# GNN edge stage: first layer summed transposed in one PSUM bank, node sums turned to 24×128

## What is computed

```python
m_input = jnp.concatenate([node_states[src], node_states[dst], edge_rel_emb], axis=-1)
h = jax.nn.relu(m_input @ W1 + b1)
messages = jax.nn.relu(h @ W2 + b2)
agg = jax.ops.segment_sum(messages, dst, num_segments=node_states.shape[0])
updated = node_states + jax.nn.relu(agg @ Wn + bn)
return _layer_norm(updated, gamma, beta)
```

## Time and profile before

| | us |
|---|---|
| median of three runs | 2293.29 |
| lowest and highest | 2289.66, 2296.72 |
| span of the profiled execution | 2166.6 |
| time of the profiled execution beside its span | not given |
| PE busy | 1892.6 (87%) |
| weight loads (PEld) busy | 1536.6 (71%) |
| DVE, ACT, POOL busy | 863.9, 647.7, 767.3 |
| edge stage, first PE work to last window addition | 622 to 1832 |

### The profile page before, as it was taken

The page is one execution under the profiler, slowest core; times in us unless marked ns, Lnnn a source line. Parts: engine busy times, 40 slices in busy tenths (PEclk is TensorE's granted clock), DMA queues, the critical chain, the costliest instruction groups (busy, mean ns, idle before and its releaser), DMA issues.

```text
span 2166.6 us, 36842 instructions
## 1 busy us (share of the span) xinstructions
PE 1892.6 (87%) x11147; PEld 1536.6 (71%) x11148; DVE 863.9 (40%) x2898; ACT 647.7 (30%) x1217; POOL 767.3 (35%) x805
## 2 busy tenths in 40 slices
PE   3777779989878888889999999999999997797796
PEld 2444454445577777779999999999999997444344
DVE  7998860123333333333333333333333332745203
ACT  4666650010023333332222222222222221610201
POOL 3000000000047777776555555555555552100000
PEclk9999979999979999995555555555555555899898
DMA  1000000010143333332222222222222222000001
GB/s 48 0 0 0 0 2 1 0 34 0 36 120 82 82 79 81 82 81 65 61 60 59 60 59 59 60 60 60 60 59 58 59 60 62 1 4 1 2 1 30
DMA packets 158346, 93.70 MB, mean 43 GB/s; under 512 B 120530, under 2 KB 143825, under 8 KB 158297
## 3 DMA queue, kind: packets, MB, share of 16 engines
q0 software_dynamic: 25088, 51.43, 8.7%
q1 hardware_dynamic: 133208, 41.60, 7.9%
HBM read 86.44 MB, written 6.52 MB: 43 GB/s over the span
## 4 chain that ended last, share of the span: by engine, by line
PE 51%; DMA 9%; issue 4%; DVE 4%; POOL 3%; ACT 1%; DVEq 1%; SPq 1%; POOLq 0%; ACTq 0%
PE ps L846 11%; PE ps L831 10%; PE ps L855 9%; DMA arena<-x_w1a,idx 8%; PE ps L724 7%; PE ps L823 5%; PE ps L839 5%; POOL arena L605 3%; PE ps L921 2%; DVE arena L1316 1%; DVE idx L1430 1%; DMA x_w1b<-arena 0%; DVE stats L1306 0%; PE ps L931 0%; PE ps L952 0%
## 5 line engine op out<-in xcount | busy, mean ns | idle before, releaser
L605 POOL DMA_INDIRECT arena<-x_w1a,idx x784 | 740.3, 944 | 1054.9 <-issue 781.8
L724 PE MATMUL ps<-adj,arena 128*128 (+2 forms) x1875 | 367.6, 358 | 14.3 <-DVE arena L1281 7.9
L846 PE MATMUL ps<-w_c,arena 128*128 128x128 f32 x1568 | 345.9, 390 | 0.0
L855 PEld LDWEIGHTS ps<-arena 128*128 128x128 f32 x1568 | 297.9, 282 | 58.8 <-ACT arena L1109 56.8
L855 PE MATMUL ps<-arena 128*128 128x24 f32 x1568 | 293.4, 334 | 41.0 <-ACT arena L1109 41.0
L1109 ACT ACTIVATE arena<-arena 128x512 f32<-128x512 f32 x196 | 123.4, 629 | 671.1 <-DVE arena L1465 671.1
L831 PE MATMUL ps<-arena 88*128 88x128 f32 x1568 | 321.9, 375 | 1.6 <-DMA arena<-x_w1b 0.9
L724 PEld LDWEIGHTS ps<-adj,arena 128*128 128x128 bf16 x1875 | 172.0, 99 | 203.1 <-issue 25.9
L831 PEld LDWEIGHTS ps<-arena 88*128 88x128 f32 x1568 | 305.2, 288 | 2.4 <-ACT arena L1100 2.4
L846 PEld LDWEIGHTS ps<-w_c,arena 128*128 128x128 f32 x1568 | 304.8, 288 | 0.4 <-ACT arena L1105 0.4
L1460 DVE TENSOR_TENSOR arena<-ps,arena 128x512 f32<-128x512 f32 x196 | 135.6, 692 | 356.9 <-DMA arena<-x_w1a,idx 225.6
(11 more groups left out here) (165 smaller groups left out, 1252.7 us busy)
## 6 DMA issues: line engine op xcount, KB each, us to landing
arena<-in_edge_attr SPq DMA_DIRECT2D x196, 128.0 KB, 2.3
arena<-x_w1a,idx POOLq DMA_INDIRECT x784
arena<-x_w1b SPq DMA_DIRECT2D x196, 12.0 KB
x_spill<-arena SPq DMA_DIRECT2D x1, 1600.0 KB, 7.8
x_w1a<-arena SPq DMA_DIRECT2D x6, 256.0 KB, 2.3
x_w1b<-arena SPq DMA_DIRECT2D x6, 256.0 KB, 2.5
arena<-x_spill SPq DMA_DIRECT2D x6, 256.0 KB, 4.6
out_x<-arena SPq DMA_DIRECT2D x3, 512.0 KB
```

The source lines that it names most:

```text
L605: pool.indirect_dma_start(out=z_e[v][:, j * D:(j + 1) * D], out_offset=None, in_=xa_d[:, :], in_offset=bass.IndirectOffsetOnAxis(ap=idx[:, ...
L724: last = pe.matmul(ps[:, u, 0:w], parts[q][:, k, :], adj[:, k, bass.ds(c0, w)], start=(k == 0 and q == 0), stop=(k == NT - 1 and q == 2))
L846: last = pe.matmul(ps[:, 5 + v % 2, j * P:(j + 1) * P], h_t[v % 2][:, j * P:(j + 1) * P], w_c[:, :], start=True, stop=True)
L855: last = pe.matmul(ps[:, 7, 0:WIN], msg[v % 2][:, j * P:(j + 1) * P], oh_e[v][:, j, :], start=(j == 0), stop=(j == J - 1))
```

## The change

In the edge stage the first layer's result is summed in PSUM, already transposed. One product with `w_e` as the stationary operand and the 512 transposed input columns as the moving one writes features × edges into one bank. Then four transpositions of the gathered rows, of the kind that the kernel already uses but with the start flag off, add to the same bank. The DVE addition and the bank for the separate transposition fall away. The wait for the gathered rows goes from DVE to PE.

The node sums are turned round: `oh_e` (24 columns) is the stationary operand and the messages (128 columns) the moving one, which gives 24×128 sums. ACT copies these out (`take_sums`), and PE turns them with one small product (`window`). DVE adds one block later than before. The inputs' transposition uses one PSUM bank in place of two. Most per-slot semaphore lists (`ec_onehot`, `ec_used`, `oh_e_ready`, `ect_out`, `h_ready`, `m_ready`, `m_sum`, `msg_ready`, `win_ready`, `win_added`, `z_ready`, `idx_ready`) become single counters; `z_sum` and `zt_ready` are gone, `sums_ready` and `sums_out` are new. The lines left out below are these declarations and one increment in `gather_index`.

```diff
--- before.py
+++ after.py
@@ -146,6 +146,7 @@
         w_e = [arena[:, 9024 + 128 * u:9152 + 128 * u] for u in range(2)]
         oh_e = [arena[:, 9280 + 96 * v:9376 + 96 * v].rearrange("p (j w) -> p j w", j=J)
                 for v in range(SLOTS)]
+        sums = [arena[0:WIN, 9792 + D * u:9792 + D * (u + 1)] for u in range(2)]
         res = [arena[:, a:a + 512].rearrange("p (j d) -> p j d", d=D) for a in (8000, 8512)]
@@ -272,10 +273,15 @@
                 eng.wait_ge(s, n)
-        def passed(eng, sems, i, v, back=0, by=1):
...
+        def passed(eng, s, i, v, back=0, by=1):
             w = v - back
-            n = by * (i + 1) if w >= 0 else by * i
-            wait_from_one(eng, sems[w % SLOTS], n)
+            if isinstance(s, list):
+                n = by * (i + 1) if w >= 0 else by * i
+                wait_from_one(eng, s[w % SLOTS], n)
+            else:
+                n = SLOTS * i + w + 1
+                if not (isinstance(n, int) and n <= 0):
+                    eng.wait_ge(s, n)
         def at(i, v):
@@ -599,7 +605,7 @@
             def gather(i, v):
                 passed(pool, idx_ready, i, v)
-                wait_from_one(pool, zt_ready[v], i)
+                passed(pool, z_ready, i, v, back=SLOTS)
                 pool.sem_inc(gather_mark, 1)
                 for j in range(J):
                     pool.indirect_dma_start(out=z_e[v][:, j * D:(j + 1) * D], out_offset=None, in_=xa_d[:, :],
@@ -818,26 +824,23 @@
             def inputs_t(i, v):
                 passed(pe, ec_loaded, i, v, by=16)
                 passed(pe, ec_onehot, i, v)
-                passed(pe, ect_out, i, v, back=2)
+                passed(pe, ect_out, i, v, back=1)
                 for j in range(J):
-                    last = pe.transpose(ps[0:KE, v % 2, j * P:(j + 1) * P], ec[v % 2][:, j, :], ident_f[:, :])
-                last.then_inc(ec_used[v], 1)
-
-            def hidden(i, v):
+                    last = pe.transpose(ps[0:KE, 0, j * P:(j + 1) * P], ec[v % 2][:, j, :], ident_f[:, :])
+                last.then_inc(ec_used, 1)
+
+            def hidden_t(i, v):
+
+                z_t = ps[:, 2 + v % 2, :]
                 passed(pe, ect_out, i, v)
                 passed(pe, w_loaded, i, v, by=16)
-                passed(pe, z_sum, i, v, back=2)
+                passed(pe, h_ready, i, v, back=2)
+                pe.matmul(z_t, w_e[v % 2][0:KE, :], ec_t[v % 2][0:KE, :], start=True, stop=False)
+                passed(pe, g_loaded, i, v, by=64)
                 for j in range(J):
-                    last = pe.matmul(ps[:, 2 + v % 2, j * P:(j + 1) * P], ec_t[v % 2][0:KE, j * P:(j + 1) * P],
-                                     w_e[v % 2][0:KE, :], start=True, stop=True)
-                last.then_inc(z_ready[v], 1)
-
-            def hidden_t(i, v):
-                passed(pe, z_sum, i, v)
-                passed(pe, h_ready, i, v, back=1)
-                for j in range(J):
-                    last = pe.transpose(ps[:, 4, j * P:(j + 1) * P], z_e[v][:, j * P:(j + 1) * P], ident_f[:, :])
-                last.then_inc(zt_ready[v], 1)
+                    last = pe.matmul(z_t[:, j * P:(j + 1) * P], z_e[v][:, j * P:(j + 1) * P], ident_f[:, :],
+                                     is_transpose=True, start=False, stop=(j == J - 1))
+                last.then_inc(z_ready, 1)
             def messages(i, v):
                 passed(pe, h_ready, i, v)
@@ -845,35 +848,43 @@
                 for j in range(J):
                     last = pe.matmul(ps[:, 5 + v % 2, j * P:(j + 1) * P], h_t[v % 2][:, j * P:(j + 1) * P], w_c[:, :],
                                      start=True, stop=True)
-                last.then_inc(m_ready[v], 1)
-
-            def window(i, v):
+                last.then_inc(m_ready, 1)
+
+            def sum_nodes(i, v):
+
                 passed(pe, msg_ready, i, v)
                 passed(pe, oh_e_ready, i, v)
+                passed(pe, sums_out, i, v, back=1)
+                for j in range(J):
+                    last = pe.matmul(ps[0:WIN, 1, 0:D], oh_e[v][:, j, :], msg[v % 2][:, j * P:(j + 1) * P],
+                                     start=(j == 0), stop=(j == J - 1))
+                last.then_inc(sums_ready, 1)
+
+            def window(i, v):
+
+                passed(pe, sums_out, i, v)
                 passed(pe, win_added, i, v, back=1)
-                for j in range(J):
-                    last = pe.matmul(ps[:, 7, 0:WIN], msg[v % 2][:, j * P:(j + 1) * P], oh_e[v][:, j, :],
-                                     start=(j == 0), stop=(j == J - 1))
-                last.then_inc(win_ready[v], 1)
+                pe.matmul(ps[:, 7, 0:WIN], sums[v % 2], ident_f[0:WIN, 0:WIN], start=True, stop=True).then_inc(win_ready, 1)
             def step(i, v, first=False, left=2):
                 if left >= 1:
-                    hidden(*at(i, v + 1))
-                hidden_t(i, v)
+                    hidden_t(*at(i, v + 1))
                 if left >= 2:
                     inputs_t(*at(i, v + 2))
                 if not first:
+                    sum_nodes(*at(i, v - 1))
+                messages(i, v)
+                if not first:
                     window(*at(i, v - 1))
-                messages(i, v)
             with pe.If_ne(flag, 0):
                 scan(pe, MLP, scan_tile)
             with pe.Else():
                 inputs_t(0, 0)
-                hidden(0, 0)
                 inputs_t(0, 1)
+                hidden_t(0, 0)
                 step(0, 0, first=True)
                 for v in range(1, SLOTS + 1):
                     step(*at(0, v))
@@ -1097,21 +1109,29 @@
             def inputs_out(i, v):
                 passed(act, ec_used, i, v)
                 passed(act, z_ready, i, v, back=2)
-                act.activation(ec_t[v % 2][0:KE, :], ps[0:KE, v % 2, :], ACT.Copy).then_inc(ect_out[v], 1)
+                act.activation(ec_t[v % 2][0:KE, :], ps[0:KE, 0, :], ACT.Copy).then_inc(ect_out, 1)
             def hidden_relu(i, v):
-                passed(act, zt_ready, i, v)
+                passed(act, z_ready, i, v)
                 passed(act, m_ready, i, v, back=2)
-                act.activation(h_t[v % 2], ps[:, 4, :], ACT.Relu, bias=cols[:, 0:1]).then_inc(h_ready[v], 1)
+                act.activation(h_t[v % 2], ps[:, 2 + v % 2, :], ACT.Relu, bias=cols[:, 0:1]).then_inc(h_ready, 1)
             def message_relu(i, v):
                 passed(act, m_sum, i, v)
-                act.activation(msg[v % 2], msg[v % 2], ACT.Relu).then_inc(msg_ready[v], 1)
-
-            def step(i, v, left=2):
-                hidden_relu(i, v)
+                act.activation(msg[v % 2], msg[v % 2], ACT.Relu).then_inc(msg_ready, 1)
+
+            def take_sums(i, v):
+                passed(act, sums_ready, i, v)
+                passed(act, win_ready, i, v, back=2)
+                act.activation(sums[v % 2], ps[0:WIN, 1, 0:D], ACT.Copy).then_inc(sums_out, 1)
+
+            def step(i, v, left=2, first=False):
+                if left >= 1:
+                    hidden_relu(*at(i, v + 1))
                 if left >= 2:
                     inputs_out(*at(i, v + 2))
+                if not first:
+                    take_sums(*at(i, v - 1))
                 message_relu(i, v)
             with act.If_ne(flag, 0):
@@ -1119,13 +1139,16 @@
             with act.Else():
                 inputs_out(0, 0)
                 inputs_out(0, 1)
-                for v in range(SLOTS):
-                    step(0, v)
+                hidden_relu(0, 0)
+                step(0, 0, first=True)
+                for v in range(1, SLOTS + 1):
+                    step(*at(0, v))
                 with act.Fori(1, NB // SLOTS - 1) as i:
-                    for v in range(SLOTS):
-                        step(i, v)
-                for v in range(SLOTS):
+                    for v in range(1, SLOTS + 1):
+                        step(*at(i, v))
+                for v in range(1, SLOTS):
                     step(NB // SLOTS - 1, v, left=SLOTS - 1 - v)
+                take_sums(NB // SLOTS - 1, SLOTS - 1)
             phase_end(act, 6)
             norms = [0]
@@ -1448,35 +1471,28 @@
             def block_start(i, v):
                 passed(dve, ec_used, i, v, back=2)
-                wait_from_one(dve, win_ready[v], i)
+                passed(dve, sums_ready, i, v, back=SLOTS)
                 rel = drel[:, bass.ds(SLOTS * i + v, 1), :].rearrange("p a j -> p j a").broadcast_to([P, J, WIN])
                 w = win_i[:, :].rearrange("p (a w) -> p a w", a=1).broadcast_to([P, J, WIN])
-                dve.tensor_tensor(ec[v % 2][:, :, R:KE], w, rel, ALU.is_equal).then_inc(ec_onehot[v], 1)
-                dve.tensor_tensor(oh_e[v], w, rel, ALU.is_equal).then_inc(oh_e_ready[v], 1)
-
-            def add_gathered(i, v):
-                passed(dve, z_ready, i, v)
-                passed(dve, g_loaded, i, v, by=64)
```

(58 more changed lines are left out.)

## The result

The changed kernel takes 2337.4 us (median of 4 runs, 2333.6 to 2339.4), the kernel before, beside it, 2291.5 us. The ratio is 1.020, interval 1.0165 to 1.0237: some 2% slower, where 15% faster was forecast. The profiled execution took 2333.6 us for a span of 2331.8; in every run of this study some 1.8 us lay around the span.

A forecast was written before the change was run, and what follows sets the result against it. Edge stage bound first by POOL's gather issue, then by PE at half clock. With the clock up: span 2166.6 − 219 − 4 − 9 = 1935, plus 12 around it, 1947 us; range 1925 to 2070.

The forecast's parts named there:

- The clock: PE in the edge stage: few clock falls, each undone within a block or two; clock near 1.0 from 640 us.
- PE's block: PE in the edge stage: 34 places for 32, 3.78 us per block at full clock, about 4.2 at upper prices.
- POOL's bound, head, tail, sum: Edge stage: 490 gathers at 1.2475 us save 219 us, head 4, tail 9; new span 1935 us.
- The waits: Edge stage: the wait for gathered rows moves to PE, no new late event; POOL's 1.25 us per gather stays the bound.
- How that stands to the median: Whole kernel: the median is 126.7 us above the profiled span; 12 us taken around the new span, giving 1947.
- Reading (a): Around the kernel: a fixed 127 us lies around any span; as a rival 2062 us, chance 0.12.
- Reading (b): Edge stage: timed runs sit at 1.2 GHz longer than the profiled one, paying 104 or 127 us more; held likelier.
- Rival 4: PE through the edge stage: clock stays at 1.2 GHz, two more places, +84 us, 2377, or 2345; chance 0.06.
- Rival 3: Edge stage: clock up only part of the time, half of 196 blocks at 7.25 us, +221 us, 2168; chance 0.06.
- Rival 2: PE's order in the edge stage exposes ACT's and DVE's answers, 5.3 us per block, +61 us, 2008; chance 0.06.

The follow-up runs named there:

- e2: Changed kernel with its 14 single counters put back to one semaphore per slot; 1942.95 us.
- e14: The kernel of e2 run again, unchanged, as base for later runs; 2307.0 us, the kernel before 2295.7 us.
- e12: The kernel of e2 with one gather per block instead of four, three quarters of the rows left out; 1814.3 us.
- e8: The changed kernel, unchanged, measured again beside the kernel before; 2316.5 us, ratio 1.008.
- e9: The changed kernel with semaphores per slot, as e2, measured again; 2301.7 us, ratio 1.002.
- e10: The kernel before, unchanged, run for its trace; 2292.75 us, ratio 0.9994.
- e18: The kernel of e2 with four gathers per block of 32 columns each instead of 128, other rows taken; 1940.0 us.
- e13: The kernel of e2 without gathers, the same bytes of fixed rows loaded by one plain DMA per block on SP; 1814.2 us.
- e16: The kernel of e12 slowed by nine small additions on POOL per block, so that PE must wait for rows; 2041.2 us.
- e17: The kernel of e13 slowed by twelve small additions on POOL per block, so that PE must wait for rows; 2097.3 us.
- e1: The kernel before, unchanged, repeated for its span and clock; 2134.3 us, runs from 2031 to 2273.

## Why the prediction was wrong

Point by point, by its own steps:

- **The clock.** Right for the quiet condition. In e2 it is 1.00 in every stretch from 700 to 1500 us, with eight transpositions in 34 places. That neither bears out nor refutes the rule of the Trainium skill (TensorE: Matmul & The Clock Gate, Part 4) that transpositions do not count as busy, since 26 places were none. That the clock stood at 0.8 in the measured kernel goes with the stalls, not with the products: e14's kernel is e2's, and its clock was 0.82 to 0.84.
- **PE's block.** 3.78 us forecast at full clock, with 4.2 as the upper price; 4.33 measured (e12). The term that was mis-sized is the start of each group: by 0.111 us a place, the 34 places are 3.78, and the six starts above leave 0.55 more, most of it behind the messages (1.09 for 8 places) and the window (0.33 for 2). The feature matmul (0.96 for 8 places) saves nothing, the sums cost 0.98 and the transpositions 0.44, as taken. The slack to 4.99 was 0.66 us instead of 1.2, and it sufficed, so the miss does not show in e2's time.
- **POOL's bound, head, tail, sum.** They came out in e2: 412 gathers take 515 us, 5.00 us per block. Head: the 17th gather starts at 632.4 us instead of 637.5, 5 us sooner where 4 was forecast. Tail: 11.5 us, forecast 8.5. The last gather ends at 1594.6, forecast 1595; span 1941.5, forecast 1935. In the measured kernel the last gather ends at 1975.9.
- **The waits.** "So the bound stays POOL's 1.25 us" is the step that failed. It holds where TensorE's increments come on time. In the late condition 44% of those recorded in the changed kernel are over 0.6 us late (median of these 2.7 us), for `z_ready`, `sums_ready`, `m_ready`, `ec_used` and `win_ready` alike. Each is a link of one loop (products, relu, messages, sums, copy, window, next gather), so a lateness that no buffer covers is paid in full: 7.0 us per block for 5.0. No row of the profile of before could show it, as that execution had none. The clue was elsewhere, in the gap below.
- **How that stands to the median.** Reading (a), a fixed 127 us around any span, is false: 1.8 us. The Trainium skill (Runtime: NRT & Kernel Launch, The ~15µs preamble/postamble breakdown) has 9 to 15 us; the 1.8 us here are below it. The 12 us that the forecast took for this were thus 10 too many. Reading (b), timed runs longer at 1.2 GHz, is half right: beside e8 and e9 the clocks are 0.70 to 0.75 in runs of 2288 to 2302 us, but in e10 and beside it 0.74 to 0.80 in runs just as long, so the time does not follow the clock. In the late condition a block takes 6.75 us at either clock [e10's stretches], so a kernel that lifts the clock wins nothing back. The 127 us were not an early fall of the clock alone but another condition than the profiled one.
- **The rivals.** Rival 4, slower, had the sign, and its 2345 us lie near the 2337 measured, but by luck: its mechanism, a low clock with PE full, did not occur. Rival 3 had a clock between the two levels, but as a cause. Rival 2 is nearest, answers in series on PE's path, but it was priced at 0.3 us per block from 1.2 us of slack; the late increments cost 2.0.

Why the change is 1 to 2% *slower* in the late condition is only argued: it has one more product of TensorE that others wait for (`sums_ready`, then the copy, then the window), so one more link that can be late, and ACT and DVE are held up by that one most often. It fits that 44% of its recorded increments are late and 26% of those of the kernel before (e10), but no run takes the link away. The per-slot version seems a little better (ratios 1.002 and 1.010 against 1.008 and 1.020), but its two intervals lie as far apart as the kernels do.

In the quiet condition the per-slot version of the changed kernel (1943 us) equals the fastest run of the one before (1942 to 2273 us) and beats all others, and its gain is the steady clock; in the late one the kernel before is 0 to 2% better. So which kernel is faster hangs on the condition.

**What stays open:** what makes a condition. The same kernel and the same chip number showed both, and nothing recorded tells what else ran on the chip. The gathers' own packets don't tell them apart: their median duration is 0.22 us in e2 and in e9. The increment is recorded late, but open is whether the semaphore or the write of the product ahead of it is at fault, since a matmul's end is modelled in the profile; PE's next groups started on time (L849 at 1178.52 above), so the products themselves were not held up. And whether bytes or number of the gathers count: e18 met the quiet condition.

## What to carry to other kernels

When the median of the timed runs and the profiled span lie far apart (here 127 us, against the 1.8 us that any run shows), the profile describes another execution than the one that is timed: repeat both before costing a change from its rows. Beside indirect gathers, be wary of adding a TensorE result that others wait for to a loop in which nothing buffers it; a buffer of a few microseconds behind each such result should help, but no run here tried it. And look at whether the rate of work follows the clock before putting a price on the clock.

## What the runs showed of the hardware

- In the late condition, with four indirect gathers per block of 7 us, 311 of 706 recorded semaphore increments of TensorE stood over 0.6 us (up to 9.5) behind their product's end, and none of DVE's or ACT's; with two gathers 28 of 813, with one or none 0 of 3025 (e12, e13, e16, e17), and 0 in the quiet condition whatever the gathers. None was late whose product ended over 2.5 us after the start of the latest gather. The Trainium skill (Perfetto Trace Analysis, Tensor Engine Instruction (MATMUL, LD_WEIGHTS)) says that the increment goes out only once PSUM has acknowledged the written bytes, and that the profile's end is an estimate before that; no run here shows which of the two is late.
- In the quiet condition one and the same kernel before, with PE busy 200.00 us in 200, stayed at a clock of 0.50 to the end of the stage (e1), and in another run had a mean of 0.94 over the whole kernel (1942 us). Its times from 1942 to 2273 us go with these mean clocks (0.94 down to 0.70).
- A 512-column f32 product cost as much as eight places of 128 columns (0.96 us at full clock in e12), and a 24-column weight load made the sums no cheaper (0.98 for eight).
